# Reordered instruction lists in the front and the grouped pass of a two-layer attention kernel, and one more scaling on ScalarE

## The chip, the cores and the metric

The kernel runs on one core of a Trainium2 chip. The core has a matrix engine (TensorE, PE in the profile), an elementwise engine (VectorE, DVE), an engine for activations with a table of functions (ScalarE, ACT), a programmable engine (GpSimd, POOL) and a queue engine that here only starts transfers (SyncE, SP). Each engine executes its own list of instructions in order, and the engines meet only at semaphores. The metric is the device time of one execution, in microseconds (us), as the median of several runs.

## The reference, cut to what matters

The input is x, 16 sequences of 64 tokens of 256 numbers, and a context of the same shape. Two layers follow, each an attention and a feed-forward part, both added to x with a gate:

```
x = x + tanh(g_xattn[0]) * attention_0(layernorm(x))       # one head of 256; q, k, v from x, softmax over 64
x = x + tanh(g_ffn[0])   * ternary_ffn(layernorm(x))       # 8-bit tokens, weights of -1, 0, 1; 256 -> 1024 -> 256
x = x + tanh(g_xattn[1]) * grouped_attention(layernorm(x), context)
x = x + tanh(g_ffn[1])   * experts(layernorm(x))           # 1 shared and 7 routed experts, top 3 of 7
```

The third line is the long one. Inside it the tokens are normalised again, divided by a scale per channel and rounded to fp8, and four products are made from them: 16 heads of 128 for a self query, 8 heads of 128 for a self key, 8 for a self value, and 16 heads for a cross query. The cross key and value come from the context. Each head of a query and each head of a key is normalised over its 128 numbers. The self and the cross attention are computed apart (scores, softmax over 64, product with the values), their 2 x 2048 results are rounded to fp8 and multiplied with an output weight of 256 x 4096. Everything is to hold in float32 except what the reference rounds itself.

## The kernel before, in words

The 1024 tokens are 8 tiles of 128 (two sequences each). The program has three stages.

**Front** (function `front`, up to about 141.5 us). Two halves of four tiles go through the first layer: normalise, project, scores, softmax, add to x, then the ternary feed-forward in chunks (`gate_up`, `hidden`, `turn_hidden`, `down`), then the normalisation for the second layer (`turn_normed`). Between these pieces TensorE computes 24 of the 32 products of the context with the key/value weight (`context(i)`), and the other engines prepare the weights of the grouped pass: DVE takes means, ACT and DVE split every weight into a high and a low part (`weights.high`, `weights.low`), GpSimd centres them.

**Grouped pass** (function `grouped_attention`). It has 16 steps n: n = 0 to 7 are the self attention of the 8 tiles, n = 8 to 15 the cross attention of the same tiles. `LAST` is 15. In step n the attention of step n runs beside the projections and normalisations of step m = n + 1. `ahead(0)` prepares step 0; `both_own(n)` is the body for n = 0 to 6, `both_cross(n)` for n = 7 to 14, and the lists after the loops are the tail with step 15 and the first expert units. Each query or key chunk i of four heads takes this way, and every arrow crosses engines:

- `project(m, c)` on PE: four heads, each product as a high and a low part.
- `sums(m, i)` on DVE (BN statistics), `add_eps(m, i)` on ACT, `rstd(m, i)` on GpSimd: the factor of each head.
- `scale(m, i)` on DVE (one tensor_tensor, L1777) or on ACT (four activations, one per head, L2034). `act_scales(n)` at L1492 names the chunks that ACT does: 0, 3, 5 in self steps, 0, 2, 3, 5 in cross steps.
- `turn(m, i)` on PE (four transposes, L2286), `keep_qk(m, i)` on ACT (L2042).

The attention of a step has two halves h: `scores(n, h)` on PE (L2299, 32 small matmuls), `less_max(n, h)` on DVE (L1783 and L1787), `exponent(n, h)` on ACT (L2052), `total(n, h)` on DVE (L1793, L1797), `normalise(n, h)` on GpSimd (L1645), `turn_p(n, h)` on PE (L2308), `keep_pT(n, h)` on ACT (L2061), `attend(n, h)` on PE (L2325), then `unload`, `clip`, `power`, `lift` on DVE (L1803 to L1819) and `fp8(n, h)` on GpSimd (L1656), whose result feeds `output_half(n, h)` on PE (L2344) in the next step; `add_x` on DVE adds it to x. Both halves use the one PSUM bank for scores, so that `scores(n, 1)` waits for `less_max(n, 0)`, and `scores(n + 1, 0)` for `less_max(n, 1)`. In self steps `key_squares` (ACT), `key_sums` (DVE) and `key_rstd` (GpSimd) also prepare the cross keys, and the low and high parts of the weights still to come are spread over the steps. `copy_tile(n + 2)` on GpSimd converts the rounded tokens of a later tile.

**Experts** (class `Experts`): 16 units of products per (expert, group of tokens); `moe.turn`, `moe.logits`, `moe.normalise`, `moe.low` and `moe.high` are its preparation, spread over the cross steps, and the first units stand in the tail. `moe.silus` uses another function table of ACT than the exponents; each switch shows as ACT_TABLE_LOAD.

What sets the order is a list of calls written out by hand for every engine, inside `block.gpsimd`, `block.vector`, `block.scalar` and `block.tensor`, once for the front and once for the grouped pass. No scheduler moves anything.

## Time and profile before

| | |
|---|---|
| median of 3 runs | 616.31 us (615.55, 616.31, 653.21) |
| profiled execution, its own time | 614.61 us |
| its span, first to last instruction | 612.9 us |
| PE busy | 562.3 us (92%) |
| DVE busy | 476.3 us (78%) |
| ACT busy | 370.6 us (60%) |
| POOL busy | 366.7 us (60%) |
| mean granted TensorE clock | 0.978 of full speed |

The span is 1.7 us shorter than the time of the same execution. In rows, a start is counted from the first instruction of the span. A bracket at the end of a row is the idle time of that engine just before the instruction, with what ended it. A row of the windows view has the stretch, its length, then the busy time and count of PE, PE's weight loads, DVE, ACT and POOL, the granted clock, the busy share of the DMA engines and GB/s. Matmuls overlap, so that the time a matmul takes from PE is the distance to the next start, not the duration printed.

### The profile page before, as it was taken

Reading aid. Unit: us, or ns where it says so; the run is one execution under the profiler, and the core shown is the slowest. Engines: PE = TensorE matmul, PEld = TensorE weight load, DVE = VectorE, ACT = ScalarE, POOL = GpSimd, SP = SyncE. Lnnn points to the kernel's source line nnn. Section 1 sums busy time; section 2 is a strip of 40 time slices with the busy share of each in tenths; the row PEclk is TensorE's granted clock in tenths of the full one; section 3 lists DMA queues with packets and bytes.
Section 4 is the critical chain, followed back from the end, with each engine's and each line's share of the span. In section 5 each row is a group of like instructions: output and inputs, shape, how many; then the busy total and the mean of one; then the engine's idle time right before and its main releaser. Section 6 shows DMA issues by size and latency. Waiting matters only on the chain.

```text
span 612.9 us, 11721 instructions
## 1 busy us (share of the span) xinstructions
PE 562.3 (92%) x4250; PEld 445.8 (73%) x4250; DVE 476.3 (78%) x980; ACT 370.6 (60%) x769; POOL 366.7 (60%) x299
## 2 busy tenths in 40 slices
PE   2999769978969999999989999999999999999996
PEld 1564324744648888888878878888887988888885
DVE  4597999877688999999998999999996845334343
ACT  1459667665965766765677767778777244533221
POOL 4101475202777778868778987777778445754331
PEclk9999899997979999999999999999999999999999
DMA  7793112114252121041194131222201001310002
GB/s 222 242 357 115 52 52 112 61 69 140 106 157 83 36 104 59 13 139 35 30 357 132 43 124 60 88 87 88 88 18 53 1 1 51 102 34 4 2 1 69
DMA packets 44569, 54.94 MB, mean 90 GB/s; under 512 B 8416, under 2 KB 30816, under 8 KB 44512
## 3 DMA queue, kind: packets, MB, share of 16 engines
q1 hardware_dynamic: 44512, 54.20, 27.1%
q8 instruction: 34, 0.56, 0.4%
q14 instruction: 23, 0.19, 0.1%
HBM read 41.60 MB, written 12.58 MB: 88 GB/s over the span
## 4 chain that ended last, share of the span: by engine, by line
PE 60%; ACT 7%; DVE 5%; issue 3%; DMA 1%; DVEq 0%; ACTq 0%
PE g_proj L2256 11%; PE g_proj L2344 9%; PE g_turn L2286 6%; PE g_scores L2299 5%; PE g_op L2325 4%; ACT g_qn L2034 3%; PE g_op L2264 3%; PE g_op L474 3%; PE g_op L475 3%; PE g_op L476 2%; PE g_proj L459 2%; PE g_proj L461 2%; PE g_proj L460 2%; ACT g_qkT L2042 1%; PE g_scores L459 1%
## 5 line engine op out<-in xcount | busy, mean ns | idle before, releaser
L1635 POOL TENSOR_TENSOR g_rs<-g_ve,neg_half 128x4 f32<-128x4 f32 x80 | 83.7, 1061 | 34.5 <-ACT g_ve L2008 34.3
L2256 PE MATMUL g_proj<-w_hi,g_xqc 128*128 128x512 f32 x192 | 85.1, 443 | 5.6 <-ACT g_qn L2034 4.2
L1656 POOL TENSOR_TENSOR g_cat<-g_yb,g_kb 128x1024 fp32r<-128x1024 bf16 x32 | 71.3, 2236 | 29.8 <-DVE g_yb L1819 29.8
L2256 PE MATMUL g_proj<-w_lo,g_xqc 128*128 128x512 f32 x192 | 76.9, 400 | 0.0
L503 POOL TENSOR_TENSOR m_h_lo<-m_h,m_h_hi 128x512 fp32r<-128x512 f32 x32 | 41.3, 1292 | 54.6 <-ACT m_h_hi L490 54.6
L1763 DVE BATCH_NORM_STATS2 g_stats<-g_proj 128x6 f32<-128x256 f32 x160 | 59.2, 418 | 12.7 <-PE g_proj L2256 12.5
L2286 PE MATMUL g_turn<-ident,g_qn 128*128 128x128 f32 x384 | 58.6, 278 | 6.9 <-ACT g_qkT L2042 4.2
L2034 ACT ACTIVATE g_qn<-g_proj,g_rs 128x128 f32<-128x128 f32 x160 | 45.5, 371 | 22.3 <-POOL g_rs L1635 12.3
L2286 PEld LDWEIGHTS g_turn<-ident,g_qn 128*128 128x128 f32 x384 | 44.5, 142 | 19.3 <-ACT g_qn L2034 9.5
L490 ACT ACTIVATE m_h_hi<-m_h 128x512 fp32r<-128x512 f32 x32 | 20.2, 631 | 53.2 <-DVE m_h L497 53.2
L2256 PEld LDWEIGHTS g_proj<-w_hi,g_xqc 128*128 128x128 f32 x192 | 37.0, 193 | 15.0 <-ACT g_qn L2034 6.7
L1323 PE MATMUL f_bank<-f_w_ctx,f_ctxT 128*128 128x512 f32 x96 | 44.0, 594 | 0.9 <-ACT f_kept L1079 0.9
L2042 ACT ACTIVATE g_qkT<-g_turn,c_lnp 128x512 f32<-128x512 f32 x48 | 37.0, 791 | 11.6 <-PE g_turn L2286 11.5
L555 POOL TENSOR_TENSOR ln_rstd<-ln_ve,neg_half 128x4 f32<-128x4 f32 x6 | 6.5, 1084 | 60.1 <-DVE ln_ve L542 60.1
L2256 PEld LDWEIGHTS g_proj<-w_lo,g_xqc 128*128 128x128 f32 x192 | 37.2, 194 | 5.9 <-issue 1.0
L2042 ACT ACTIVATE g_qkT<-g_turn,x_lnp 128x512 f32<-128x512 f32 x48 | 37.7, 785 | 5.1 <-PE g_turn L2286 5.0
L513 DVE SCALAR_TENSOR_TENSOR x_res<-g_op,m_we,x_res 128x256 f32<-128x256 f32 x64 | 27.8, 479 | 16.3 <-PE g_op L476 16.3
L1645 POOL TENSOR_TENSOR g_ex<-g_ex,g_rc 128x512 f32<-128x512 f32 x32 | 33.4, 1043 | 11.2 <-DVE g_rc L1797 11.2
L2299 PE MATMUL g_scores<-g_qkT 128*64 128x64 f32 x1024 | 37.6, 228 | 1.4 <-DVE g_ex L1787 1.4
L2299 PEld LDWEIGHTS g_scores<-g_qkT 128*64 128x64 f32 x1024 | 33.2, 140 | 7.6 <-issue 5.8
L2325 PEld LDWEIGHTS g_op<-g_pT,g_v 64*128 64x128 f32 x512 | 31.1, 187 | 10.2 <-issue 7.8
L2325 PE MATMUL g_op<-g_pT,g_v 64*128 64x128 f32 x512 | 37.2, 285 | 1.4 <-ACT g_pT L2061 1.4
(243 smaller groups left out, 1664.8 us busy)
## 6 DMA issues: line engine op xcount, KB each, us to landing
kvx_rows<-f_kept SPq DMA_DIRECT2D x24, 256.0 KB, 2.4
g_ksq<-kvx_rows SPq DMA_DIRECT2D x8, 512.0 KB, 4.9
g_kraw<-kvx_rows SPq DMA_DIRECT2D x16, 256.0 KB, 3.1
g_v<-kvx_rows SPq DMA_DIRECT2D x8, 512.0 KB, 4.3
m_raw<-in_L_W SPq DMA_DIRECT2D x16, 256.0 KB, 3.2
c_raw<-in_L_wqT SPq DMA_DIRECT2D x4, 512.0 KB, 5.8
f_w_ctx<-in_L_wkvxT SPq DMA_DIRECT2D x4, 512.0 KB, 7.7
c_praw<-in_L_wprojT SPq DMA_DIRECT2D x4, 512.0 KB, 5.2
```

The source lines that it names most:

```text
L503: self.nc.gpsimd.tensor_tensor(self.h_lo[n % 2][:, f, :], self.h[:, f, :], self.h_hi[n % 2][:, f, :].bitcast(F32), ALU.subtract).then_inc( ...
L1323: last = T.matmul(context_bank(e)[:], ctxT[:, c_, tile * P:(tile + 1) * P], w_ctx[:, chunk, c_, :], start=c_ == 0, stop=c_ == KT - 1)
L1635: G.tensor_tensor(rs[:, at % NORMS, :], ve[:, at % NORMS, :], k["half"][:, 0:4], ALU.pow).then_inc(q["rs_done"], 1)
L1656: G.tensor_tensor(cat[:, h].rearrange("p h (b s) -> p b h s", b=2), yb[:, h, :].rearrange("p (b h s) -> p b h s", b=2, s=SEQ), kb[:, h, :] ...
L1763: last = V.bn_stats(stats[:, at % NORMS, two, :], heads)
L2034: last = A.activation(qn[:, i % 2, h * D:(h + 1) * D], source[:, h * D:(h + 1) * D], ACT.Copy, scale=by[:, h:h + 1])
L2042: A.activation(qkT[:, n % 2, at:at + 4, :], turns[TURN_BANK[i]][:].rearrange("p (h m) -> p h m", h=4), ACT.Identity, bias=lnp[:, w + 1:w + ...
L2256: last = T.matmul(bank(n, i)[:], xqc[:, n % 2, view * KT + c_, :], w[:, c_, :], start=c_ == 0 and part == 0, stop=c_ == KT - 1 and part == 1)
L2286: last = T.transpose(out, qn[:, i % 2, h * D:(h + 1) * D], k["ident"][:])
L2299: last = T.matmul(sp_[at, (g * 2 + b) * SEQ:(g * 2 + b + 1) * SEQ], qkT[:, n % 2, 2 * kv + b, at], qkT[:, n % 2, HEADS + kv, rows], start= ...
L2325: last = T.matmul(op[:, b, g * P:(g + 1) * P], v[rows, n % 2, kv * D:(kv + 1) * D], pT[rows, h, g, :], start=True, stop=True)
L2344: last = T.matmul(proj[OUT_BANK][:, 0:E], cat[:, h, hd % (2 * GH), :], w[hd // 4][:, hd % 4, :], start=hd == 0 and part == 0, stop=hd == H ...
```

## The change

Nothing computed differs. The lists of all four compute engines are written in another order, in the front, in `ahead`, `both_own`, `both_cross` and in the tail; and `scale(m, 2)`, the third query chunk of the 8 self tiles, goes from DVE (one instruction) to ACT (four). The core of the diff: the chunk moved, VectorE's and TensorE's lists of a self step, and ScalarE's tail.

```diff
         def act_scales(n):
-            return (0, 2, 3, 5) if cross(n) else (0, 3, 5)
+            return (0, 2, 3, 5) if cross(n) else (0, 2, 3, 5)
...
                 def both_own(n):
                     m = n + 1
+                    if n == 0:
+                        late_tokens(2)
                     less_max(n, 0)
                     sums(m, 0)
-                    if n == 0:
-                        late_tokens(2)
                     sums(m, 1)
+                    total(n, 0)
+                    if n % 2 == 0:
+                        ctx.low(dve, n // 2)
                     if n % 2 == 1:
                         ctx.mean(dve, (n + 1) // 2)
+                    key_sums(n)
+                    scale(m, 1)
                     less_max(n, 1)
-                    if n % 2 == 0:
-                        ctx.low(dve, n // 2)
-                    total(n, 0)
-                    scale(m, 1)
+                    sums(m, 2)
                     if n > 0:
                         add_x(n - 1)
-                    key_sums(n)
-                    sums(m, 2)
+                    total(n, 1)
                     sums(m, 3)
-                    total(n, 1)
-                    scale(m, 2)
+                    sums(m, 4)
                     unload(n, 0)
-                    sums(m, 4)
                     clip(n, 0)
                     sums(m, 5)
                     power(n, 0)
...
                 def both_own(n):
                     m = n + 1
@@ -2382,48 +2383,48 @@
                     if n > 0:
                         output_half(n - 1, 0)
                         output_half(n - 1, 1)
+                    turn(m, 0)
                     project(m, 2)
                     project(m, 3)
                     turn_p(n, 0)
-                    turn(m, 0)
+                    turn(m, 1)
                     project(m, 4)
                     attend(n, 0)
-                    turn(m, 1)
+                    turn_p(n, 1)
+                    project(m, 5)
                     turn(m, 2)
-                    project(m, 5)
-                    turn_p(n, 1)
+                    attend(n, 1)
                     project(m, 6)
-                    attend(n, 1)
                     turn(m, 3)
+                    turn(m, 4)
                     project(m, 7)
-                    turn(m, 4)
 
...
-                keep_qk(LAST, 3)
-                keep_qk(LAST, 4)
-                moe.silus(act, 0, 0)
-                keep_qk(LAST, 5)
                 act.wait_ge(q["qkv_done"], projected(LAST, 5))
                 moe.high(act, 6)
+                keep_qk(LAST, 3)
                 moe.high(act, 7)
+                keep_qk(LAST, 4)
+                moe.high(act, 8)
+                keep_qk(LAST, 5)
                 exponent(LAST, 0)
-                moe.high(act, 8)
                 exponent(LAST, 1)
                 keep_pT(LAST, 0)
+                moe.exponent(act, 0)
+                moe.silus(act, 0, 0)
+                moe.silus(act, 0, 1)
                 moe.hidden_high(act, 0, 0)
-                moe.silus(act, 0, 1)
-                moe.exponent(act, 0)
                 moe.silus(act, 1, 0)
                 keep_pT(LAST, 1)
+                moe.keep(act, 5, turns[0])
```

VectorE in self step n = 2, from the first `less_max` (L1783, L1787; w_lo at L202 is the low part of a weight for a later step). Before:

```order
L1783 TENSOR_REDUCE g_mx<-g_scores 128x8
L1787 TENSOR_TENSOR g_ex<-g_scores,g_mx 128x512
L1763 BN_STATS g_stats<-g_proj 128x6 x4
L1783 TENSOR_REDUCE g_mx<-g_scores 128x8
L1787 TENSOR_TENSOR g_ex<-g_scores,g_mx 128x512
L202 SCALAR_TENSOR_TENSOR w_lo<-x_raw_58,x_sc,w_hi 128x512 x2
L1793 TENSOR_REDUCE g_sm<-g_ex 128x8
L1797 RECIPROCAL g_rc<-g_sm 128x8
L1777 TENSOR_TENSOR g_qn<-g_proj,g_rs 128x512
L1852 SCALAR_TENSOR_TENSOR x_res<-g_proj,c_coef,x_res 128x256
L1770 TENSOR_REDUCE g_kve<-g_ksq 128x8
```

and with the change:

```order
L1783 TENSOR_REDUCE g_mx<-g_scores 128x8
L1787 TENSOR_TENSOR g_ex<-g_scores,g_mx 128x512
L1763 BN_STATS g_stats<-g_proj 128x6 x4
L1793 TENSOR_REDUCE g_sm<-g_ex 128x8
L1797 RECIPROCAL g_rc<-g_sm 128x8
L202 SCALAR_TENSOR_TENSOR w_lo<-x_raw_58,x_sc,w_hi 128x512 x2
L1770 TENSOR_REDUCE g_kve<-g_ksq 128x8
L1777 TENSOR_TENSOR g_qn<-g_proj,g_rs 128x512
L1783 TENSOR_REDUCE g_mx<-g_scores 128x8
L1787 TENSOR_TENSOR g_ex<-g_scores,g_mx 128x512
L1763 BN_STATS g_stats<-g_proj 128x6 x2
L1852 SCALAR_TENSOR_TENSOR x_res<-g_proj,c_coef,x_res 128x256
```

The second `less_max` moves behind `total(2,0)`, the weight, the key sums (L1770) and `scale(3,1)` (L1777); it stood right behind the four statistics.

TensorE at the end of cross step n = 13, from the last matmul of a projection to the scores of the next step (L2286 `turn`, L2308 `turn_p`, L356 the transposes of the experts' tokens, L2325 `attend`, L2299 `scores`). Before:

```order
L2256 MATMUL g_proj<-w_lo,g_xqc 128x512
L2286 MATMUL g_turn<-ident,g_qn 128x2x64 x4
L2308 MATMUL g_turn<-ident,g_ex 128x128 x4
L2286 MATMUL g_turn<-ident,g_qn 128x128 x4
L356 MATMUL g_proj<-ident,m_xn 128x128 x2
L2325 MATMUL g_op<-g_pT,g_v 128x128 x8
L2299 MATMUL g_scores<-g_qkT 64x64 x16
```

and with the change, where every line number of TensorE is one higher:

```order
L2257 MATMUL g_proj<-w_lo,g_xqc 128x512
L2309 MATMUL g_turn<-ident,g_ex 128x128 x4
L356 MATMUL g_proj<-ident,m_xn 128x128 x2
L2287 MATMUL g_turn<-ident,g_qn 128x2x64 x4
L2326 MATMUL g_op<-g_pT,g_v 128x128 x8
L2287 MATMUL g_turn<-ident,g_qn 128x128 x4
L2300 MATMUL g_scores<-g_qkT 64x64 x16
```

`turn(14,3)` goes behind `attend(13,1)`, and `turn(14,2)` behind `turn_p(13,1)` and the experts' transposes.

ScalarE in the tail, from the exponents of step 15 (L2052) on (L484 silu, L400 the experts' exponent, L2061 `keep_pT`, L490 the high part of a hidden chunk). Before:

```order
L2052 ACT_TABLE_LOAD
L2052 ACTIVATE g_ex<-g_ex 128x512
L318 ACTIVATE m_w_hi_1519<-m_raw_1529 128x512
L2052 ACTIVATE g_ex<-g_ex 128x512
L2061 ACTIVATE g_pT<-g_turn 128x512
L490 ACTIVATE m_h_hi_1542<-m_h 128x512
L484 ACT_TABLE_LOAD
L484 ACTIVATE m_silu<-g_scores 128x512
L400 ACT_TABLE_LOAD
L400 ACTIVATE m_lg<-m_lg 128x28
L484 ACT_TABLE_LOAD
L484 ACTIVATE m_silu<-g_proj 128x512
```

and with the change, where line numbers of the pass are one lower:

```order
L2051 ACTIVATE g_ex<-g_ex 128x512 x2
L2060 ACTIVATE g_pT<-g_turn 128x512
L400 ACTIVATE m_lg<-m_lg 128x28
L484 ACT_TABLE_LOAD
L484 ACTIVATE m_silu<-g_proj 128x512
L484 ACTIVATE m_silu<-g_scores 128x512
L490 ACTIVATE m_h_hi_1542<-m_h 128x512
L484 ACTIVATE m_silu<-g_proj 128x512
L2060 ACTIVATE g_pT<-g_turn 128x512
```

Both exponents of step 15 and the experts' exponent stand together, and one table load is left of the four in this piece; the one ahead of the first silu, some rows earlier, is gone too, since that silu now stands here.

In the front the moves are smaller: `context(22)` goes from before `turn_hidden(1, 3)` and the last two `down` to behind them, `turn(1)` ahead of `scores(0)`, and the means, scales and low parts that prepare weights stand at other places between the chunks of DVE. At n = 0 the output weight's first high and low parts stand first on ACT and GpSimd, and `late_tokens(2)` first on DVE. On GpSimd `copy_tile(n + 2)` goes in self steps from behind `rstd(m, 1)` to behind `rstd(m, 5)`, and `normalise(n, 1)` ahead of `rstd(m, 3)`. The DMA queue's list is as before.

## Rows read from the trace of the kernel before

**Rows 1.** Page of the profile, part 1: busy time, share, instructions.

```profile
PE 562.3 (92%) x4250; PEld 445.8 (73%) x4250; DVE 476.3 (78%) x980; ACT 370.6 (60%) x769; POOL 366.7 (60%) x299
```

**Rows 2.** Windows view, self tiles: busy us (and count) by engine.

```profile
240.00:280.00 40.00, 39.64 (x383) 33.30 (x382) 37.80 (x75) 26.52 (x64) 32.13 (x26) 1.00 0.20 68
```

**Rows 3.** Timeline of TensorE (start, us, engine): scores(n,0), n = 1,7,8,10,15.

```profile
191.67 1.03 PE L2299 MATMUL g_scores<-g_qkT 128*64 128x64 f32 x28
...
312.91 0.80 PE L2299 MATMUL g_scores<-g_qkT 128*64 128x64 f32 x20
...
333.12 1.09 PE L2299 MATMUL g_scores<-g_qkT 128*64 128x64 f32 x30
...
368.37 0.85 PE L2299 MATMUL g_scores<-g_qkT 128*64 128x64 f32 x21
...
454.61 0.57 PE L2299 MATMUL g_scores<-g_qkT 128*64 128x64 f32 x12
```

**Rows 4.** Timeline of TensorE, n = 2: turn_p(2,0), turn, attend(2,0), turn_p(2,1), project.

```profile
222.40 0.60 PE L2308 MATMUL g_turn<-ident,g_ex 128*128 128x128 f32 x4
222.83 0.60 PE L2286 MATMUL g_turn<-ident,g_qn 128*128 128x128 f32 x4
...
224.29 1.16 PE L2325 MATMUL g_op<-g_pT,g_v 64*128 64x128 f32 x16
...
227.24 0.60 PE L2308 MATMUL g_turn<-ident,g_ex 128*128 128x128 f32 x4
227.93 0.50 PE L2256 MATMUL g_proj<-w_hi,g_xqc 128*128 128x512 f32 x1
```

**Rows 5.** Timeline of VectorE, n = 2: less_max(2,1), scale(3,1), scale(3,2).

```profile
216.73 0.69 DVE L1783 TENSOR_REDUCE g_mx<-g_scores 128x8 f32<-128x512 f32 x1 [0.21 <-PE g_scores L2299]
...
220.36 0.69 DVE L1777 TENSOR_TENSOR g_qn<-g_proj,g_rs 128x512 f32<-128x512 f32 x1
...
225.00 0.69 DVE L1777 TENSOR_TENSOR g_qn<-g_proj,g_rs 128x512 f32<-128x512 f32 x1 [0.26 <-POOL g_rs L1635]
```

**Rows 6.** Timeline of GpSimd, n = 2: fp8 of step 1, rstd(3,0..1).

```profile
213.34 4.62 POOL L1656 TENSOR_TENSOR g_cat<-g_yb,g_kb 128x1024 fp32r<-128x1024 bf16 x2 [1.56 <-DVE g_yb L1819]
217.92 2.41 POOL L1635 TENSOR_TENSOR g_rs<-g_ve,neg_half 128x4 f32<-128x4 f32 x2
```

**Rows 7.** Timeline of ScalarE, n = 2: scale(3,0).

```profile
218.95 1.14 ACT L2034 ACTIVATE g_qn<-g_proj,g_rs 128x128 f32<-128x128 f32 x4 [1.58 <-POOL g_rs L1635]
```

**Rows 8.** Timeline of TensorE, cross step n = 12: turn_p(12,1), turn(13,3).

```profile
416.92 0.60 PE L2308 MATMUL g_turn<-ident,g_ex 128*128 128x128 f32 x4
418.07 0.63 PE L2286 MATMUL g_turn<-ident,g_qn 128*128 128x128 f32 x4 [0.55 <-ACT g_qkT L2042]
```

**Rows 9.** Timeline of VectorE, same step: sums(13,4).

```profile
414.10 0.76 DVE L1763 BATCH_NORM_STATS2 g_stats<-g_proj 128x6 f32<-128x256 f32 x2 [0.95 <-PE g_proj L2256]
```

**Rows 10.** Waits of TensorE: releaser, total us, times, longest.

```profile
PE g_proj L2256 <- ACT g_qn L2034: 4.2, 1, 4.2
...
PE g_turn L2286 <- ACT g_qn L2034: 2.2, 1, 2.2
```

**Rows 11.** Lines view, power step L1813: ns min/median/max.

```profile
L1813 DVE TENSOR_SCALAR g_kb<-g_yb x32: 407/427/2254, 187.9 to 476.2; 128x1024 uint16<-128x1024 uint16 x32
```

**Rows 12.** Timeline of ScalarE, tail: table load, exponent(15,0).

```profile
460.93 1.28 ACT L2052 ACT_TABLE_LOAD   x1
462.22 0.63 ACT L2052 ACTIVATE g_ex<-g_ex 128x512 f32<-128x512 f32 x1
```

**Rows 13.** Timeline of TensorE, tail: attend(15,1).

```profile
473.27 1.16 PE L2325 MATMUL g_op<-g_pT,g_v 64*128 64x128 f32 x16 [1.35 <-ACT g_pT L2061]
```

**Rows 14.** Timeline of TensorE, front's end: context(21) with (22), turn_normed(1).

```profile
124.48 3.70 PE L1323 MATMUL f_bank<-f_w_ctx,f_ctxT 128*128 128x512 f32 x8
...
136.64 1.94 PE L1332 MATMUL f_bank<-ident,f_xn 128*128 128x128 f32 x8 [3.90 <-DVE f_xn L547]
```

**Rows 15.** Lines view, weights.low L202 of the self weights.

```profile
L202 DVE SCALAR_TENSOR_TENSOR w_lo<-c_raw,c_sc,w_hi x16: 736/746/2846, 47.2 to 158.2; 128x512 fp32r<-128x512 f32 x16
```

More of the change, by code:

```diff
@@ L1408, in _ @@
             down(1, 3)
+            context(22)
             context(23)
@@ L1725, in _ @@
                     both_cross(n)
+                moe.rstd(pool, 5)
+                normalise(LAST, 0)
                 moe.low(pool, 6)
-                normalise(LAST, 0)
                 moe.low(pool, 7)
+                moe.rest(pool, 4)
+                normalise(LAST, 1)
                 moe.low(pool, 8)
-                normalise(LAST, 1)
                 moe.hidden_low(pool, 0, 0)
-                moe.rest(pool, 4)
-                moe.rstd(pool, 5)
                 fp8(LAST, 0)
+                moe.rest(pool, 5)
+                fp8(LAST, 1)
                 moe.hidden_low(pool, 0, 1)
-                fp8(LAST, 1)
-                moe.rest(pool, 5)
                 moe.rstd(pool, 6)
@@ L2112, in both_own @@
                     m = n + 1
-                    add_eps(m, 0)
+                    if n == 0:
+                        own_out.high(act, 0)
+                    exponent(n, 0)
                     if n == 0:
                         split_query(0)
-                        own_out.high(act, 0)
+                    add_eps(m, 0)
+                    add_eps(m, 1)
+                    key_squares(n)
+                    scale(m, 0)
+                    if n == 0:
+                        own_out.high(act, 1)
@@ new lines, in both_own @@
+                    keep_qk(m, 0)
+                    exponent(n, 1)
+                    add_eps(m, 2)
+                    keep_pT(n, 0)
+                    keep_qk(m, 1)
+                    scale(m, 2)
+                    add_eps(m, 3)
+                    keep_pT(n, 1)
+                    add_eps(m, 4)
+                    scale(m, 3)
+                    add_eps(m, 5)
+                    keep_qk(m, 2)
+                    if n in (1, 3, 5):
+                        split_query((n + 1) // 2)
@@ new lines, in both_own, with both_cross @@
+                    scale(m, 5)
+                    keep_qk(m, 3)
+                    keep_v(m, 0)
+                    keep_v(m, 1)
+                    keep_qk(m, 4)
+                    keep_qk(m, 5)
+                def both_cross(n):
+                    m = n + 1
+                    if cross(n):
+                        keep_qk(n, 3)
+                        keep_qk(n, 4)
+                    scale(m, 0)
+                    if n in MATRIX:
+                        moe.high(act, MATRIX[n])
+                    if cross(n):
+                        keep_qk(n, 5)
@@ L2128, in both_own @@
+                    scale(m, 2)
+                    exponent(n, 1)
+                    if n in (TILES - 1, TILES):
+                        ctx_out.high(act, 2 * (n - TILES + 1) + 1)
+                    keep_pT(n, 0)
                     keep_qk(m, 1)
```

422 lines of the change are left out of this document (190 added, 232 removed).

## The prediction

> **What bounds the kernel now.** I read the page's busy shares first: TensorE is busy 562.3 us of the 612.9 us span, 92%, VectorE 78% [rows 1]. An average over a front, 16 attention steps and a long run of expert products tells little about a reordering, so the second view is that by windows. In a stretch of self steps TensorE is busy 39.64 of 40 us, and VectorE 37.80 [rows 2]: two engines close to full at once, ScalarE with a third of its time free (26.52). The reader should see that neither can be relieved far: whatever VectorE is spared, TensorE stands right behind it. The third view is the step itself, by the starts of the scores on TensorE [rows 3]: n = 1 to 6 take (312.91 - 191.67) / 6 = 20.21 us each, n = 7 20.21, n = 8 and 9 (368.37 - 333.12) / 2 = 17.63, n = 10 to 14 (454.61 - 368.37) / 5 = 17.25. The fourth is the waits. A wait of TensorE shows as idle time, or only as a longer distance between two starts: behind `turn_p(2,0)` the next start comes 0.43 us later, behind `turn_p(2,1)` 0.69 [rows 4], so 0.26 us are lost there though no row calls it idle.
>
> **The sum** is made against the profiled execution, 614.6 us (1.7 us of it outside the span); the median of the runs shown is 616.3, so my number stands 1.7 us lower than one made against the median. The experts behind the tail are not touched.
>
> **Front: -2.5.** `context(21)` and `(22)` start at 124.48 as 8 matmuls, 3.70 us; one context is half, about 1.75 once the overlap is left out [rows 14]. They stand ahead of `turn_hidden(1,3)` and `down`, whose result goes through `add_ffn` and the normalisation before TensorE can do `turn_normed(1)`; there TensorE idles 3.90 us. With `context(22)` behind the last `down` it fills that idle time: -1.75. The other moves in VectorE's list put weight means and scales into waits that it has; I take -0.75 for all of them. The bounds are wide: -5.5 if the whole 3.90 is filled too, and +4 if moved VectorE steps land beside GpSimd's large operations. Such a step, one piece of `weights.low`, takes 0.746 us in the median and took 2.846 at worst [rows 15]: 2.1 us lost in one meeting, and two more of them make +4.
>
> **`ahead`: 0** (plus or minus 1). TensorE runs nearly without a break there, and the moves change who is ready early.
>
> **n = 0: -1.5.** The only wait of a projection for ScalarE is 4.2 us long [rows 10], here, for `scale(1,0)`. Before, `late_tokens(2)` stands on VectorE between `sums(1,0)` and `sums(1,1)`, and ScalarE does `add_eps(1,1)` ahead of `scale(1,0)`; with `late_tokens(2)` first, it fills VectorE's wait for the scores instead. But then everything of step 0 on VectorE comes later, and `rstd(1,0)` stands behind a weight part on GpSimd. So most of the stall remains: I take a third of it, between +2 and -4.2.
>
> **Self steps 1 to 6: -2.7.** Two things go. The 0.26 us behind `turn_p(n,1)` was `project(m,6)` waiting for ScalarE's `scale(m,3)`; now `project(m,5)` and `attend(n,1)` stand between [rows 4]. And VectorE loses `scale(m,2)`, 0.69 us and a wait of 0.26 for GpSimd's rstd in front of it [rows 5], which costs ScalarE 1.14 [rows 7], with 13 us in 40 free. VectorE's work is 37.80 / 40 x 20.21 = 19.1 us in a step, and comes to 18.4; TensorE then sets the step. If only the visible wait goes, a step gains 0.26, if VectorE had set it, 0.69; the middle, 0.45, times 6. Bounds 0 to -4. `scale(m,2)` has to be done before `project(m,5)` may overwrite its bank: ScalarE does it directly behind `keep_qk(m,1)`, and by adding the pieces I find it done only about 0.4 us early.
>
> **n = 7: 0.** TensorE waits 2.20 us once for `scale(8,0)` on ScalarE [rows 10], whose input is loaded back by DMA; the DMA list is as before. Bounds +1, -2.2.
>
> **Cross steps 10 to 14: -3.5.** Behind `turn_p(12,1)` the next start comes 1.15 us later instead of 0.43, of which 0.55 is shown idle, since `turn(13,3)` waits for a `keep_qk` just being done [rows 8]. Now `turn(m,3)` stands behind `attend(n,1)`. VectorE waits 0.95 us in the same step for `project(13,4)` [rows 9]; `moe.normalise` now stands there. I take 0.7, by the distance of starts (0.72), times 5; bounds 0 and -4.75 (0.95 each).
>
> **n = 8 and 9: -2.4.** The same 0.7, and 0.5 for what makes these steps 0.4 longer than the others: a power step that takes 0.427 us in the median and 2.254 at most [rows 11] meets GpSimd's low part of the output weight, which moves. Bounds 0 and -1.8 each.
>
> **Tail: -2.0.** From `scores(15,0)` at 454.61 to the end of `attend(15,1)` at 474.43 it takes 19.8 us [rows 3, 13], more than a step that also projects. ScalarE's five table loads there become one. A load takes 1.28 us [rows 12], so 5.1 us of ScalarE go. TensorE shows 1.35 us idle at `attend(15,1)` for `keep_pT` [rows 13], which stood behind three of the loads. I take that and half of the load ahead of `exponent(15,0)`; bounds 0 and -3. Here a rule can be weighed. The row shows that the exponent starts 0.01 us after the load ends [rows 12]. The Trainium skill, "ScalarE: Activation LUTs", section "What ACT_TABLE_LOAD costs", has 1.28 us for the load and 1.38 for a drain, 2.66 together for each switch: by it ScalarE would be spared 10.6 us, and the tail would go to its end of the range, -3, the time to 601. The trace agrees with the first part and shows nothing of the second, so I keep to the row.
>
> **Allowance: +2.0.** The new order puts chains closer together, in 14 steps. VectorE shows waits of 0.21 and 0.26 us in one step as it is [rows 5]; I add some 0.15 per step for new ones on TensorE.
>
> Sum: -2.5 - 1.5 - 2.7 - 2.4 - 3.5 - 2.0 + 2.0 = -12.6. **614.6 - 12.6 = 602.0 us.**
>
> **Rivals.**
>
> *A. Only the waits that show go away* (0.20). The self steps gain 0.26 x 6 = 1.6, the seven cross steps 0.55 x 7 = 3.9, the tail 1.35; the rest is taken back by waits elsewhere: 607.8 us. For it: a step with two engines at 95% and more [rows 2] gives little to a new order.
>
> *B. The front grows* (0.08). For it: one meeting with GpSimd cost 2.1 us, and VectorE's list there is long and much of it moved. Two new ones make +4 in place of -2.5: 602.0 + 6.5 = 608.5 us. The Trainium skill, "SBUF — State Buffer", section "Who interferes with whom", says that a VectorE instruction with two SBUF inputs and GpSimd share a port pair by an exclusive lock, and that the order of issue decides who is blocked: by that rule any reordering draws these meetings anew, which speaks against counting on a gain. [Rows 15] and the 2.254 us of [rows 11] agree with it.
>
> *C. A closed loop in the self step becomes the bound, and the kernel slower* (0.08). `less_max(n,1)` moves behind `total(n,0)`, the key sums and `scale(m,1)`. In n = 2 it started at 216.73, 4.8 us into the step (which begins at 191.67 + 20.21 = 211.88); behind `scale(3,1)`, which started at 220.36, it starts 4.3 us later [rows 5], while `turn_p(n,1)` is called 1.8 us earlier, right behind `attend(n,0)` (224.29 + 1.1) [rows 4]. And `scale(m,1)` waits for GpSimd: the fp8 pair of the step before, 4.62 us, then two rstd, 2.41, end at 220.33 [rows 6]. So fp8, rstd, `scale(m,1)`, `less_max(n,1)`, softmax, `attend(n,1)` and fp8 form a ring that closes once per step. GpSimd's part and the scale are 7.7 us; the dozen instructions behind them, at 0.4 to 1.2 us each by the rows of their kinds, I estimate at 9.7, and with what stands between in the queues at 11.6: 19.3, just under TensorE's 19.8. With 0.2 us more at each hand-over the ring takes 22.2, and the six steps lose 2.0 each, +12; the cross steps, which have a like ring, gain nothing, and with front, n = 0 and tail as above it comes to 614.6 + 12 - 6.0 = 620.6 us. The kernel gets slower from a self step of about 21.9 on, where 6 x 1.7 eats the 9.9 us of the other terms.
>
> *D. More than forecast* (0.14): no new waits (-2.0), self steps at 0.69 (-1.4), cross steps at 0.95 (-1.25), another 1.5 at n = 0: 595.9 us.
>
> **Chances and range.** The forecast (597 to 607 by its bounds) has 0.50, the rivals the chances above. The range from 595 to 613 leaves out C and what lies past D, or between A and no change. About 2%, 12.3 us, is taken here as what tells a change from none; against the median that is faster than 604.0. The forecast lies just below that line: of its 0.50 I count 0.36 faster, with D 0.50. Same: 0.47, from A (0.20), B (0.08), the rest of the forecast (0.14) and most of C. Slower than 628.6 needs C and a longer front together: 0.03.
>
> **What would show it.** Self steps of about 19.8 between starts of scores, cross steps of 16.5, no idle row before `turn(m,3)`; `attend(15,1)` some 17.5 to 18 us after `scores(15,0)`, and six table loads in all; the grouped pass beginning some 2.5 us earlier; at n = 0 a wait of 2.5 to 4 still there. If TensorE shows waits at `turn_p(n,1)` for GpSimd's normalised exponents, C has come; if self steps stay at 20.2 with waits at new places, A. The prediction is most easily wrong in the front, whose meetings of VectorE and GpSimd I can't place.

## The result and the profile after

The changed kernel takes 596.29 us (median of 4 runs, 595.50 to 596.84), the kernel before 615.93 (median of 4): a ratio of 0.9687, with a 95% interval of 0.9666 to 0.9708. The ratio leaves out one slow run of the kernel before, 653.21 us. The change makes it 3.1% faster. The time lies inside the range of the prediction (595 to 613), 1.3 us from its lower end, 5.7 us below the number forecast (602.0) and next to rival D (595.9). The profiled execution took 595.50 us, 6.5 less than the forecast made against such an execution; its span is 593.8, its mean granted clock 0.990, where it was 0.978.

By stage, from the first matmul of the pass and the starts of `scores(n,0)` in both traces; the forecast's number stands beside it:

| stage | before | after | difference | forecast |
|---|---|---|---|---|
| front, to the first matmul of the pass | 141.54 | 134.74 | -6.8 | -2.5 |
| `ahead` | 25.84 | 25.32 | -0.5 | 0 |
| n = 0 | 24.29 | 21.78 | -2.5 | -1.5 |
| n = 1 to 6 | 121.24 | 118.64 | -2.6 | -2.7 |
| n = 7 | 20.21 | 18.38 | -1.8 | 0 |
| n = 8 and 9 | 35.25 | 33.93 | -1.3 | -2.4 |
| n = 10 to 14 | 86.24 | 83.77 | -2.5 | -3.5 |
| from `scores(15,0)` to the end | 158.29 | 157.24 | -1.05 | -2.0 |
| allowance | | | | +2.0 |
| sum | 612.9 | 593.8 | -19.1 | -12.6 |

The starts of the scores on TensorE in the changed kernel (start, duration, engine), n = 1, 7, 8, 10 and 15, answer to [rows 3]:

```profile
181.84 1.15 PE L2300 MATMUL g_scores<-g_qkT 128*64 128x64 f32 x32
...
300.48 1.15 PE L2300 MATMUL g_scores<-g_qkT 128*64 128x64 f32 x32
...
318.86 1.15 PE L2300 MATMUL g_scores<-g_qkT 128*64 128x64 f32 x32
...
352.79 1.15 PE L2300 MATMUL g_scores<-g_qkT 128*64 128x64 f32 x32
...
436.56 1.15 PE L2300 MATMUL g_scores<-g_qkT 128*64 128x64 f32 x32
```

The self steps take (300.48 - 181.84) / 6 = 19.77 us, where it was 20.21, and n = 10 to 14 take (436.56 - 352.79) / 5 = 16.75, where it was 17.25. In the windows view (stretch, length, busy time of PE, PE's weight loads, DVE, ACT, POOL, then the clock) the same 40 us as in [rows 2]:

```profile
240.00:280.00 40.00, 40.00 (x389) 34.16 (x388) 37.86 (x74) 30.49 (x74) 33.53 (x27) 1.00 0.20 67
```

TensorE has no idle time left in a self step, 40.00 of 40 us. ScalarE is busy 4 us more than before, VectorE the same, in slightly more steps (40 / 19.77 = 2.02 instead of 1.98). TensorE's waits of the whole kernel (releaser, total, times, longest), first one of the kernel before, then the changed kernel's, against [rows 10]:

```profile
PE f_bank L1280 <- DVE f_h L863: 8.1, 6, 2.9
```

```profile
PE f_bank L1204 <- DVE f_an L547: 10.7, 2, 9.4
PE g_turn L2287 <- ACT g_qn L2033: 6.1, 3, 3.8
...
PE f_bank L1332 <- DVE f_xn L547: 2.2, 1, 2.2
PE f_bank L1280 <- DVE f_h L863: 1.7, 2, 1.1
```

The 4.2 us at n = 0 are 3.8 now (the largest of the second row). The wait of the front for VectorE's hidden chunks (L1280 for f_h), 8.1 us in 6 places before, which the prediction did not look at, is 1.7. At the ends of the cross step n = 13 and of the front, TensorE's timeline, against [rows 8] and [rows 14]:

```profile
418.05 1.16 PE L2326 MATMUL g_op<-g_pT,g_v 64*128 64x128 f32 x16
419.14 0.66 PE L2287 MATMUL g_turn<-ident,g_qn 128*128 128x128 f32 x4
419.73 1.15 PE L2300 MATMUL g_scores<-g_qkT 128*64 128x64 f32 x32
```

```profile
129.95 1.32 PE L1332 MATMUL f_bank<-ident,f_xn 128*128 128x128 f32 x8 [2.19 <-DVE f_xn L547]
134.74 3.75 PE L2265 MATMUL g_op<-f_w_ctx,f_ctxT 128*128 128x512 f32 x4 [3.48 <-PEq L57]
```

`turn(14,3)` at 419.14 follows `attend(13,1)` with no idle row: the 0.55 us are gone. In the front the wait at `turn_normed(1)` fell from 3.90 to 2.19, but, as e8 shows, that is not what brought the 6.8 us. The tail, ScalarE and then TensorE, against [rows 12] and [rows 13]:

```profile
445.03 0.63 ACT L2051 ACTIVATE g_ex<-g_ex 128x512 f32<-128x512 f32 x1 [2.29 <-DVE g_ex L1787]
...
446.69 1.28 ACT L484 ACT_TABLE_LOAD   x1
447.98 0.60 ACT L484 ACTIVATE m_silu<-g_proj 128x512 f32<-128x512 f32 x1
```

```profile
453.57 1.16 PE L2326 MATMUL g_op<-g_pT,g_v 64*128 64x128 f32 x16
```

The one load left stands behind the exponents. `attend(15,1)` has no wait ahead of it and ends 18.2 us after `scores(15,0)` started (19.8 before). The kernel has six table loads in all, as forecast, where it had ten. Last, VectorE's two steps that met GpSimd (ns, min/median/max), against [rows 11] and [rows 15]:

```profile
L1813 DVE TENSOR_SCALAR g_kb<-g_yb x32: 407/427/566, 178.2 to 456.5; 128x1024 uint16<-128x1024 uint16 x32
```

```profile
L202 DVE SCALAR_TENSOR_TENSOR w_lo<-c_raw,c_sc,w_hi x16: 734/746/2326, 57.0 to 154.8; 128x512 fp32r<-128x512 f32 x16
```

The worst power step is 0.566 instead of 2.254; the worst low part still 2.326. Some meetings of the two engines went, some came.

### The profile page after: what moved, and what is told of

The parts are those of the page before. It is cut to its first block, busy times and chain, and to the rows that moved or that the text cites. A ratio compares the mean times of both kernels' runs of the same rounds, so it can differ in the third digit from the quotient of the medians.

```text
span 593.8 us, 11742 instructions
## 1 busy us (share of the span) xinstructions
PE 554.6 (93%) x4250; PEld 442.7 (75%) x4250; DVE 469.5 (79%) x972; ACT 379.6 (64%) x797; POOL 366.6 (62%) x299
## 4 chain that ended last, share of the span: by engine, by line
PE 66%; DVE 4%; POOL 2%; issue 2%; ACT 1%; DVEq 0%; POOLq 0%
PE g_proj L2257 14%; PE g_proj L2345 10%; PE g_turn L2287 6%; PE g_op L2326 5%; PE g_scores L2300 5%; PE g_op L2265 3%; PE g_op L474 2%; PE g_op L475 2%; PE g_op L476 2%; PE g_proj L459 2%; PE g_proj L461 2%; PE g_proj L460 2%; PE g_turn L2309 2%; PE g_turn L459 1%; PE g_scores L459 1%
## 5 line engine op out<-in xcount | busy, mean ns | idle before, releaser
L1635 POOL TENSOR_TENSOR g_rs<-g_ve,neg_half 128x4 f32<-128x4 f32 x80 | 86.6, 1092 | 33.5 <-ACT g_ve L2007 32.6
L1656 POOL TENSOR_TENSOR g_cat<-g_yb,g_kb 128x1024 fp32r<-128x1024 bf16 x32 | 70.9, 2224 | 24.7 <-DVE g_yb L1819 24.7
L2033 ACT ACTIVATE g_qn<-g_proj,g_rs 128x128 f32<-128x128 f32 x192 | 54.9, 372 | 22.7 <-POOL g_rs L1635 12.6
L2287 PE MATMUL g_turn<-ident,g_qn 128*128 128x128 f32 x384 | 57.4, 278 | 6.1 <-ACT g_qn L2033 6.1
L490 ACT ACTIVATE m_h_hi<-m_h 128x512 fp32r<-128x512 f32 x32 | 20.3, 633 | 49.2 <-DVE m_h L497 49.2
L474 PE MATMUL g_op<-m_w_hi,m_h_hi 128*128 128x256 f32 x128 | 36.3, 284 | 0.0
```

The costliest lines, as they stand in the source:

```text
L474: self.nc.tensor.matmul(out, hi, w_hi[:, f, :], start=f == 0, stop=False)
L1635: G.tensor_tensor(rs[:, at % NORMS, :], ve[:, at % NORMS, :], k["half"][:, 0:4], ALU.pow).then_inc(q["rs_done"], 1)
L1656: G.tensor_tensor(cat[:, h].rearrange("p h (b s) -> p b h s", b=2), yb[:, h, :].rearrange("p (b h s) -> p b h s", b=2, s=SEQ), kb[:, h, :] ...
L2033: last = A.activation(qn[:, i % 2, h * D:(h + 1) * D], source[:, h * D:(h + 1) * D], ACT.Copy, scale=by[:, h:h + 1])
L2287: last = T.transpose(out, qn[:, i % 2, h * D:(h + 1) * D], k["ident"][:])
```

## The experiments

All ratios are to the kernel before, timed beside the experiment on the same chip; the changed kernel stands at 0.9687. Where two experiments are compared in microseconds of whole time, the difference is that of their ratios, times 615 us.

**e1 to e4, one stage each.** Each is the kernel before with the new lists of one stage:

```diff
 e1_front   lists of front():                     new      ahead, both_own, both_cross, tail:  as before
 e2_self    lists of ahead and both_own:          new      front, both_cross, tail:            as before
-           return (0, 2, 3, 5) if cross(n) else (0, 3, 5)
+           return (0, 2, 3, 5) if cross(n) else (0, 2, 3, 5)
 e3_cross   lists of both_cross:                  new      front, ahead, both_own, tail:       as before
 e4_tail    lists behind the loops over the steps: new     all others:                         as before
```

> The kernel before with the new lists of the front alone (VectorE, ScalarE, TensorE, GpSimd up to the start of the grouped pass). Theory A, each stage keeps its own gain: the pass begins 6.8 us earlier, as in the trace of the changed kernel, and nothing follows, so 6.8 us less in all (ratio 0.989), with self steps at 20.2 and cross steps at 17.3. Theory B, the front's gain is partly given back or multiplied by what the pass then meets: more than 1.5 us away from that.

> The kernel before with the new lists of ahead and of the self steps, and the third query chunk on ScalarE; front, cross steps and tail as before. Theory A: ahead -0.5, n = 0 -2.5, n = 1 to 6 -2.6, together -5.6 us (ratio 0.991), and n = 7 at 20.2 as before, since its list is that of the cross steps. Theory B, the granted clock at n = 7 hangs on what the self steps leave behind: n = 7 at 18.4 too, -7.4 us.

> The kernel before with the new lists of the cross steps (n = 7 to 14) alone. Theory A: n = 7 -1.8, n = 8 and 9 -1.3 together, n = 10 to 14 -2.5, in all -5.6 us (ratio 0.991), and the granted clock stays at 1.0 through n = 7, where it was 0.79 before from 318 to 326 us. Theory B, the clock's gain at n = 7 needs the new self steps: n = 7 at about 20.2, in all -3.8 us.

> The kernel before with the new lists of the tail alone (step 15 and the first expert units), four table loads of ScalarE fewer. Theory A: -1.0 us, the two waits of TensorE there. Theory B, as forecast, the loads are on the way and -2.0 or more. Theory C: the new order of the tail needs the cross steps that end earlier, and gives nothing here.

| | median us | ratio, 95% interval | its stage in the trace |
|---|---|---|---|
| e1_front | 605.82 | 0.9855 (0.9840 to 0.9870) | pass begins at 135.51 |
| e2_self | 608.97 | 0.9906 (0.9887 to 0.9925) | self steps 19.77, n = 0 21.76 |
| e3_cross | 610.97 | 0.9936 (0.9921 to 0.9951) | n = 8, 9: 16.92, 16.87; then 16.75 |
| e4_tail | 613.52 | 0.9978 (0.9969 to 0.9988) | -1.4 from `scores(15,0)` on |

The four ratios multiplied give 0.968, the changed kernel's: the stages add up. But not each as theory A had it. e4's 1.4 lies between theory A (1.0) and B (2.0), and C is out. e2 gained 5.8 us as theory A said, though in its trace n = 7 takes 18.72, as theory B said. e3 gained 3.9 us, not 5.6: 1.05 at n = 7, 1.5 at n = 8 and 9, 2.5 at n = 10 to 14, the last two as in the changed kernel or a little more; against that its front, with the lists as before, ended 0.6 later, and step 0 began 0.9 later. e1 gained 8.9, not 6.8, which is theory B: the front gave 6.0, and 2.8 came at n = 0 (22.90 instead of 24.29) and n = 7 (18.82 instead of 20.21), whose lists are as before. These 2.8 are the granted clock, as the rows show. The step n = 7 in the windows view, for the kernel before, e1, e2 and e8; then TensorE's wait in that step in e2, and its second scores in that step in the kernel before and in e2:

```profile
312.90:333.10 20.20, 17.45 (x173) 15.07 (x172) 17.38 (x34) 14.99 (x33) 13.91 (x11) 0.92 0.66 213
```

```profile
305.62:324.44 18.82, 15.99 (x174) 13.69 (x173) 17.19 (x34) 15.01 (x33) 13.94 (x11) 1.00 0.70 231
```

```profile
307.59:326.31 18.72, 16.02 (x173) 13.69 (x173) 16.58 (x33) 14.89 (x33) 14.03 (x12) 1.00 0.63 198
```

```profile
312.36:332.81 20.45, 17.43 (x173) 15.05 (x172) 17.37 (x34) 15.10 (x33) 14.14 (x11) 0.92 0.65 212
```

```profile
PE g_turn L2287 <- ACT g_qn L2032: 2.0, 1, 2.0
```

```profile
322.03 1.86 PE L2299 MATMUL g_scores<-g_qkT 128*64 128x64 f32 x32
```

```profile
315.92 1.15 PE L2300 MATMUL g_scores<-g_qkT 128*64 128x64 f32 x32
```

The list of n = 7 is the same in these four kernels and the wait nearly so: 2.0 us in e2, 2.2 before [rows 10], 2.5 in e8. The granted clock of the step is 0.92 in two of them (the kernel before and e8) and 1.00 in the others, and the step takes 20.2 and 20.45 us in the first, 18.8 and 18.7 in the others. In the kernel before, the wait ends at 318.76, and half clock (1.2 GHz) lasts from about 320.2 to 323.6: the same scores take 1.86 us in it and 1.15 at 2.4 GHz. So of the 1.8 us at n = 7 some 1.4 to 1.5 are the clock, and 0.3 to 0.4 are the new lists (18.72 in e2, 18.38 in the changed kernel, both at 1.00). With the self steps in the old order ahead of it, in e3, the new list of n = 7 takes 19.16 at full clock, longer than the old one there (18.82, e1). For n = 0 the same holds, behind a wait of 4.2 us before and of 4.5 in e1, with one list; the third row is the changed kernel's, with its new list:

```profile
167.38:191.67 24.29, 19.27 (x162) 14.86 (x161) 19.64 (x38) 15.34 (x36) 18.66 (x14) 0.86 0.52 164
```

```profile
161.43:184.33 22.90, 17.77 (x161) 13.70 (x160) 19.53 (x38) 15.38 (x36) 18.64 (x14) 0.93 0.55 173
```

```profile
160.06:181.84 21.78, 17.63 (x162) 14.29 (x161) 19.12 (x35) 17.39 (x42) 17.36 (x13) 0.92 0.49 156
```

At about the same clock as e1 the new list of n = 0 takes 1.1 us less, so of the 2.5 us there some 1.4 are the clock.

Theory B of e2, that the self steps' list makes the difference, falls with e1.

**e5, the third query chunk back on VectorE.** The changed kernel, with

```diff
-            return (0, 2, 3, 5) if cross(n) else (0, 2, 3, 5)
+            return (0, 2, 3, 5) if cross(n) else (0, 3, 5)
...
                     total(n, 1)
+                    scale(m, 2)
                     sums(m, 3)
...
                     keep_qk(m, 1)
-                    scale(m, 2)
```

> The changed kernel with the third query chunk of the self steps scaled on VectorE again, behind total(n,1); all lists else as changed. Theory A, TensorE sets the changed self step: VectorE's 18.7 us of work in a step become 19.3, still under the step's 19.8, so the steps stay at 19.8 and the time within 1 us of the changed kernel's. Theory B, VectorE's chains set it: the steps go back to about 20.2, 3 us more in all.

Measured: 600.28 us, ratio 0.9767 (0.9750 to 0.9785), by the ratios 4.9 us more than the changed kernel. Two self steps in the windows view:

```profile
204.63:224.75 20.12, 20.00 (x193) 16.81 (x192) 19.43 (x38) 13.87 (x33) 15.63 (x13) 1.00 0.31 106
224.75:244.55 19.80, 19.80 (x194) 16.81 (x193) 18.95 (x38) 14.51 (x33) 17.03 (x14) 1.00 0.10 27
```

The step with the low part of a weight on VectorE takes 20.12, that without it 19.80. VectorE is busy 19.43 us of the first. That it is in the way there is concluded from this share: no idle row of TensorE in these steps names it. The chunk on ScalarE is worth 0.33 in every second step, 1.0 in six. `ahead` and n = 0, where the chunk is back on VectorE too, are 1.0 and 0.7 longer. The rest of the 4.9 is not the chunk's: n = 7 ran in part at half clock again (19.88), and the front, with the lists of the changed kernel, ended 1.3 later. Both theories held for half of the steps.

**e6, `less_max(n,1)` back.** The changed kernel, with

```diff
                     sums(m, 1)
+                    less_max(n, 1)
                     total(n, 0)
...
                     scale(m, 1)
-                    less_max(n, 1)
```

> The changed kernel with less_max(n,1) of the self steps back ahead of total(n,0), as before. Theory A: neither place is on the way, the steps stay at 19.8 and the time within 1 us. Theory B, its new place is what gives the self steps their 0.45 us (total(n,0) and turn_p(n,0) come earlier): steps of 20.2 or more, 3 us or more in all. Theory C, the ring feared in the prediction already costs something: steps shorter than 19.8.

Measured: 600.88 us, ratio 0.9782 (0.9765 to 0.9798). The self steps take 20.48 and 20.00 in turn, 0.47 more in the mean. TensorE's timeline in step 1:

```profile
192.96 0.50 PE L2257 MATMUL g_proj<-w_hi,g_xqc 128*128 128x512 f32 x1 [0.44 <-DVE g_qn L1777]
```

Theory B. With `less_max(n,1)` ahead, VectorE comes to `scale(m,1)` later, and TensorE waits for it before the projection that overwrites its bank; the row stands in steps 1, 3 and 5, and the other steps are 0.23 longer without an idle row. The new place is worth the whole 0.45 us of a self step, 2.8 in six. The rest of the 5.8 by which e6 is slower lies at n = 7 (20.54, at clock 0.92) and in a front that ended 0.6 later. No step got shorter, so the ring of rival C costs nothing.

**e7, VectorE's front list back.** The changed kernel with the list of `front()` in `block.vector` as before; no other line.

> The changed kernel with VectorE's list of the front as before; ScalarE, TensorE, GpSimd of the front and all of the pass as changed. Theory A, VectorE's order gives the front its 6.8 us, by fewer long meetings with GpSimd and fewer waits: the pass begins at about 141 us instead of 134.7, 6 us more in all. Theory B, the others' lists give it: the pass begins at 135 to 137. Theory C, the lists fit only together: worse than the kernel before, past 143.

Measured: 612.07 us, ratio 0.9964 (0.9944 to 0.9985). The pass begins late:

```profile
150.32 3.75 PE L2265 MATMUL g_op<-f_w_ctx,f_ctxT 128*128 128x512 f32 x4 [3.01 <-PEq L57]
```

150.3 is 15.6 us behind the changed kernel and 8.8 behind the kernel before. Theory C: VectorE's old list doesn't fit the others' new ones, so VectorE's list has no share of its own in the 6.8 us. Which of the moves clash is not shown: VectorE's instructions are 2.9 us longer beside GpSimd than in the kernel before (16.5 against 13.6, counted as in e9 below), which leaves most of the 8.8 open.

**e8, `context(22)` alone.** The kernel before, with

```diff
             context(21)
-            context(22)
             turn_hidden(1, 3)
             down(1, 2)
             down(1, 3)
+            context(22)
             context(23)
```

> The kernel before with one step moved, context(22) on TensorE from ahead of turn_hidden(1,3) to behind the last down. Theory A, the step of the prediction: the pass begins 1.75 us earlier, at 139.8. Theory B, the end of the front hangs on VectorE's rounding and ScalarE's copies, not on TensorE: less than 0.5 us earlier.

Measured: 614.36 us, ratio 0.9990 (0.9969 to 1.0011). The pass begins at 142.16, 0.6 later than in the kernel before. The end of the front on TensorE:

```profile
125.65 1.88 PE L1323 MATMUL f_bank<-f_w_ctx,f_ctxT 128*128 128x512 f32 x4
128.03 1.14 PE L1294 MATMUL f_bank<-ident,f_h 128*128 128x128 f32 x8 [0.51 <-ACT f_hT L1072]
129.84 1.91 PE L1306 MATMUL f_bank<-f_values,f_hT 128*128 128x256 bf16 x16 [0.66 <-DVE x_res L895]
131.59 3.60 PE L1323 MATMUL f_bank<-f_w_ctx,f_ctxT 128*128 128x512 f32 x8
137.37 1.53 PE L1332 MATMUL f_bank<-ident,f_xn 128*128 128x128 f32 x8 [2.19 <-DVE f_xn L547]
```

Theory B. The 1.75 us that the context freed turned into two new waits at once: `turn_hidden(1,3)` waits 0.51 for ScalarE's copy and `down` 0.66 for VectorE's add to free its bank. The wait at `turn_normed(1)` shrank from 3.90 to 2.19 only because the context now stands in front of it.

**e9 and e10, GpSimd's large products cut to an eighth.** The kernel before and the changed kernel, with

```diff
-                G.tensor_tensor(h[:, s, j, :], h[:, s, j, :], lnw[:], ALU.mult)
+                G.tensor_tensor(h[:, s, j, 0:D], h[:, s, j, 0:D], lnw[:, 0:D], ALU.mult)
...
-                G.tensor_tensor(heads, heads, bcast(ctx_sums[:, n, :], 2, D), ALU.subtract)
+                G.tensor_tensor(heads[:, 0:1], heads[:, 0:1], bcast(ctx_sums[:, n, 0:1], 2, D), ALU.subtract)
```

and the same for the centring of the self weights. Both kernels leave out part of the computation.

> The kernel before, with GpSimd's large products of the front (the weighing of the hidden chunks, L750, the centring of the self weights, L185, and of the context weights, L755) done on an eighth of their columns; every wait, signal and order stays, part of the computation is left out. Theory A, the front's gain is VectorE meeting GpSimd less: some 12 us of lengthened VectorE instructions go, and the pass begins at about 135 instead of 141.5. Theory B, the gain is in the waits that the order fills, and the lengthened instructions stand beside other waits: the pass begins at 140 or later.

> The changed kernel with the same products on an eighth of their columns. Theory A: it has only some 6 us of lengthened instructions left in the part that counts, so the pass begins at 132 to 134 and the distance to the kernel before done likewise shrinks from 6.5 us to 2 or less. Theory B: the distance stays at about 6.

Measured: e9 602.91 us, ratio 0.9798 (0.9784 to 0.9813), the pass begins at 133.34, 8.2 us earlier than in the kernel before; e10 594.24, ratio 0.9644 (0.9619 to 0.9670), at 131.78, 3.0 earlier than in the changed kernel. The distance between the two, 6.8 us as they are, is 1.6 without the meetings, which thus account for 5.2 of it. Theory A. It could also be that other engines waited for GpSimd's long products themselves; they did not: the idle time that GpSimd ended on VectorE in the front is 2.5 us in each of the four traces, and on TensorE and ScalarE there is none. Set against the shortest of its kind in all traces, VectorE has 12 lengthened instructions beside GpSimd in the front before, 13.6 us too long in all, and 8 in the changed kernel, 9.5 us (3.4 of them in the first 12 us); in e10 3 are left, 2.0 us, in e9 none. The low part of the self weights (lines view) and TensorE's wait for hidden chunks in e9, whose lines are one higher:

```profile
L203 DVE SCALAR_TENSOR_TENSOR w_lo<-c_raw,c_sc,w_hi x16: 734/743/749, 47.8 to 149.6; 128x512 fp32r<-128x512 f32 x16
```

```profile
PE f_bank L1281 <- DVE f_h L864: 1.4, 3, 0.6
```

No low part takes over 0.749 us any more, and the wait of 8.1 us is 1.4, in the old order. How such a meeting reads in the trace, first VectorE and GpSimd in the kernel before, then VectorE's same instruction in the changed kernel:

```profile
71.26 1.94 DVE L856 TENSOR_SCALAR f_du<-f_am,tern_mean 128x4 f32<-128x4 f32 x1
```

```profile
68.90 2.42 POOL L750 TENSOR_TENSOR f_h<-f_h,f_lnw 128x1024 f32<-128x1024 f32 x1 [2.60 <-ACT f_junk L1064]
71.28 1.90 POOL L755 TENSOR_TENSOR f_w_ctx<-f_w_ctx,f_ctx_sums 128x1024 f32<-128x1024 f32 x1
```

```profile
64.74 0.23 DVE L856 TENSOR_SCALAR f_du<-f_am,tern_mean 128x4 f32<-128x4 f32 x1
```

An instruction on 4 numbers per partition takes 1.94 us beside GpSimd's product and 0.23 alone. It ends when GpSimd's instruction ends (73.2). The Trainium skill, "SBUF — State Buffer", section "Who interferes with whom", calls this an exclusive lock of a port pair that a tensor_scalar can take as well as an instruction with two SBUF inputs, while a tensor_reduce never does on this chip. The trace agrees with both halves: the eight reductions of L868 take 1206 ns in the mean before, six of them beside GpSimd instructions, and 1204 after, all eight beside them.

**e11 and e12, a version that might beat both.** The changed kernel with three moves against the waits left (e12: and a fourth):

```diff
-            weights.mean(dve, 0)
             ln.apply(dve, 0, lambda j: an[:, 0, j, :])
+            weights.mean(dve, 0)
...
-            add_ffn(0)                      # e12 only
             round_hidden(1, 0)
+            add_ffn(0)                      # e12 only
...
-                    if n == 0:
-                        own_out.low(pool, 0)
                     rstd(m, 0)
                     rstd(m, 1)
+                    if n == 0:
+                        own_out.low(pool, 0)
...
+                    if n == TILES - 1:
+                        turn(n, 5)
                     project_context(m, 1)
```

and on ScalarE at n = 0 `split_query(0)` behind `add_eps(m, 1)` and `key_squares(n)` behind `scale(m, 0)`.

> The changed kernel with three moves against the waits that are left: VectorE's first apply ahead of the first weight mean, as before (TensorE's first transposes done at 10.5 instead of 12.9); at n = 0 add_eps ahead of the query split, scale(1,0) ahead of key_squares and rstd ahead of the output weight's low part (its stall 3.8 to about 2.4); at n = 7 turn(7,5) ahead of the two context projections (stall 2.0 to about 0.7). Theory A: -2.4 - 1.4 - 1.3 = -5.1 us against the changed kernel, a ratio of about 0.960 to the kernel before. Theory B, VectorE takes the first one back before 60 us, since its list is the bound there: -2.7, ratio 0.964.

> The same three moves and a fourth: round_hidden(1,0) ahead of add_ffn(0) on VectorE, as before, into the wait of 1.26 us for TensorE's down. Theory A: -0.7 more. Theory B, what follows add_ffn(0) is on the way and comes 0.7 later: no gain.

Measured: e11 596.25 us, ratio 0.9694 (0.9678 to 0.9709), e12 596.32, ratio 0.9691 (0.9677 to 0.9706): no gain. Neither theory of e11 came true; e12's fourth move did as its theory B said. The first move brought about 1 us (the pass begins at 133.59 and 133.46), `turn(8,0)` waits 1.2 at n = 7 instead of 2.0, but the step takes 18.32, only 0.06 less. At n = 0 it went wrong. TensorE, VectorE and GpSimd of e11 there:

```profile
166.29 0.66 PE L2290 MATMUL g_turn<-ident,g_qn 128*128 128x128 f32 x4 [2.67 <-ACT g_qn L2033]
...
170.59 0.80 PE L2260 MATMUL g_proj<-w_hi,g_xqc 128*128 128x512 f32 x1 [2.27 <-DVE g_qn L1777]
```

```profile
165.25 3.55 DVE L202 SCALAR_TENSOR_TENSOR w_lo<-x_raw,x_sc,w_hi 128x512 fp32r<-128x512 f32 x2 [0.77 <-ACT w_hi L195]
```

```profile
165.43 2.83 POOL L231 TENSOR_TENSOR p_lo<-c_praw,p_hi 128x1024 fp32r<-128x1024 f32 x1
```

The first wait is 2.67, as hoped, but a second of 2.27 comes for `scale(1,1)`: the output weight's low part, moved behind rstd, now stands beside VectorE's `w_lo`, which takes 3.55 us for two instead of some 1.5. The step takes 23.7 us instead of 21.8. It is the meeting of the front once more, made by my own move.

## Why the prediction was right, and where it was not

The direction and the range held; the self steps came out at 19.77 where 19.8 was forecast. That the time came no further from the forecast is in part luck, since misses of both signs met: the front gave 4.3 us more than its term, 1.3 past its bound of -5.5, and the clock some 2.8 that the prediction did not contain; the cross steps gave 2.1 less and the tail 1.0. Term by term:

- **Front, -2.5.** Mis-sized, and by the wrong mechanism. `context(22)`, -1.75 in the sum, is worth nothing measurable in the old lists (e8). What the sum put at -0.75 with a range to +4, other places for VectorE's instructions and with them other meetings with GpSimd, is what counted: the meetings account for 5.2 of the 6.8 us (e9, e10). Rival B named the mechanism, the price of one meeting (2.1 us) and the doubt, but let it only lengthen the front. A reordering draws the meetings anew in both directions: counted as in e9, VectorE's instructions are 13.6 us too long before, 9.5 in the changed kernel and 16.5 in e7. The sign was in the waits view: TensorE waited 8.1 us in 6 places for hidden chunks, a row I had left out of the sum; with the meetings gone and the old order kept it is 1.4 (e9). In rival B, the Trainium skill's rule is given for instructions with two SBUF inputs, and the power step of [rows 11] is set beside it; that one is a tensor_scalar with one such input, so that only [rows 15] bears on the rule as given there (what the section has on a tensor_scalar stands at e9).
- **n = 0, -1.5.** Measured -2.5, by other means than forecast. The stall was to lose a third of its 4.2 us and lost 0.4; some 1.4 of the 2.5 are the clock (e1), which the prediction does not contain. With the old list the step took 22.5 to 24.4 us in six traces, with the new one 21.8 to 22.4 in four.
- **Self steps, -2.7.** Right in size (-2.6), half right in the reason. The chunk moved to ScalarE is worth 1.0 (e5), the place of `less_max(n,1)` 2.8 (e6); they overlap, since to undo either is enough to lengthen the steps. The 0.26 us behind `turn_p(n,1)` were a symptom: in e6 `project(m,5)` and `attend(n,1)` stand between as in the changed kernel, and the steps take 20.24 all the same.
- **n = 7, 0.** Measured -1.8, 1.4 to 1.5 of it granted clock, which fell behind the wait of 2 us in some traces and not in others with the same list. The wait itself stayed, as said.
- **Cross steps, -5.9.** Mis-sized: -3.8. The idle row, 0.55, was the better measure (0.5 a step) than the distance of starts (0.72): behind `turn(14,3)` the next start still comes 0.59 us later, where behind `turn_p(2,0)` it is 0.43 [rows 4]. n = 8 and 9 gained only 0.66 each (1.2 forecast), 0.16 more than the others. The two long power steps (2.25 us each) did go, but were not worth the 0.5 put on them, and what they met was another instruction than I named, `fp8` (L1656), which starts as the low part ends:

```profile
335.42 2.25 DVE L1813 TENSOR_SCALAR g_kb<-g_yb 128x1024 uint16<-128x1024 uint16 x1
```

```profile
332.61 2.50 POOL L231 TENSOR_TENSOR w_lo<-x_praw,w_hi 128x1024 fp32r<-128x1024 f32 x1
335.06 2.33 POOL L1656 TENSOR_TENSOR g_cat<-g_yb,g_kb 128x1024 fp32r<-128x1024 bf16 x1
```

- **Tail, -2.0.** Mis-sized: -1.6 to `attend(15,1)`, -1.05 to the end, where the experts' list takes 0.6 back. By e4 it is 0.2%. The wait at `attend(15,1)` (1.35) went; of the half load put on top of it (0.64), 0.3 shows there. The one load left takes 1.28 us, and the next activation starts 0.01 us after its end. The drain of 1.38 us behind a load, which the Trainium skill gives ("ScalarE: Activation LUTs", section "What ACT_TABLE_LOAD costs"), shows neither there nor in the gain, which stayed under the 3 us that the prediction put on it.
- **Allowance, +2.0.** Not needed as a term of its own: TensorE has no idle row over 0.1 us at n = 1 to 6 and 10 to 14. Its new waits, 1.5 us in all, stand at n = 7 to 9 and are in the differences there.
- **Rivals.** A (only visible waits) is refuted by the self steps, though its 3.9 us for the cross steps came out (3.8). C's ring stays under the bound (e6). D came nearest in time, but through the front and the clock, which it did not contain.

## What to carry to other kernels

Where VectorE and GpSimd both work through long lists, look in the trace for short VectorE instructions that last 1 to 2.5 us and end with a GpSimd instruction: VectorE's own waits do not show them (2.5 us for GpSimd in this front, against 13.6 us of lengthening), and a reordering moves them, for better or worse. Moving one engine's list alone can cost more than the whole reordering gains (e7). An instruction on the critical engine, moved out of the way, may be worth only the distance to the next thing that is late, which is seen only after the move (e8, e11).
